# A transformer block in split fp32: the weights' low parts are no longer made, and the flags that skip their products come from the raw weights

## Chip, cores and metric

One NeuronCore of a Trainium2 chip runs the whole program. The metric is device time in microseconds from launch to end; three runs of the kernel before stand in the table further down. Engines are called by these names: TensorE (PE, with its weight loads as PEld), VectorE (DVE), ScalarE (ACT), GpSimd (POOL), SyncE (SP, which here only issues transfers).

## The reference

Eight sequences of 256 tokens of width 128 pass through an attention and a gated feed-forward network, each with a layer norm before and after:

```python
x = x + layernorm(attention(layernorm(x), W_qkv))          # one head of width 128
h = silu(z @ w1.T * s1) * (z @ w2.T * s2)                   # z = layernorm(x); 128 -> 512
h = gelu(h @ h1.T * sh1)                                    # 512 -> 512, exact gelu
h = gelu(h @ h2.T * sh2)                                    # 512 -> 512
x = x + layernorm(h @ w3.T * s3)                            # 512 -> 128
```

All data is fp32. The five weight matrices of the feed-forward network hold only -1, 0 and 1; their scales are separate vectors.

## The kernel before

The 2048 tokens are 16 tiles of 128, in four blocks of four tiles (512 tokens). TensorE multiplies at its fast fp32 format (`float32r` in the code), which keeps only the upper bits of an operand. So each fp32 operand is split: `hi` is the value rounded to that format, `lo` is the rest. A product is then hi x hi + hi x lo + lo x hi, accumulated in PSUM.

For the five feed-forward matrices (`w12` is w1 and w2 side by side, then `h1`, `h2`, `w3`) ScalarE makes the `hi` parts by a copy that rounds (`weights_hi`, line 337), and GpSimd makes the `lo` parts by subtraction (`weights_lo`, line 213): one instruction of 1024 columns for `w12`, four of 512 for `h1`, four of 512 for `h2`, one of 512 for `w3`. ScalarE then sums the absolute values of each `lo` matrix by row (`sum_of_lo`, line 343). TensorE adds the rows up (`sum_flags`, line 716), VectorE copies the totals from PSUM (`copy_flags`, line 602), and TensorE reads each total into a register (`read_flag`). Where the register is zero, `ffn_product` jumps over the matmuls with `w_lo`. With weights of -1, 0 and 1 the `lo` parts are all zero, so this branch is never entered with the given inputs.

Each engine has its own list of instructions, written out by hand, and runs it strictly in order; semaphores tie the lists together. What matters around the change is the start, before the four blocks reach a steady rhythm:

- GpSimd: the inverse square roots of the layer norms (line 198) and the `lo` parts of the weights alternate. First the root for block 0's input norm, then `w12`; the root for block 1's, then four slices of `h1`; the root for block 0's attention norm, two slices of `h2`; the root for block 0's second norm, then two slices of `h2` and `w3`.
- VectorE: the statistics of block 0 and 1 (lines 437 to 446), their normalised tiles (456), the `lo` parts of activations (433), the attention output of block 0 (487 to 501), its normalised tiles `xn2` (456 again), the copy of the first two flags (602), then block 0's gates (515, 523).
- ScalarE: the `hi` parts of activations (260, 294) with the `hi` parts of weights and the four sums between them. The sums of `w12` and `h1` stand before block 0's `x2T`; those of `h2` and `w3` stand after block 0's silus and ahead of block 1's exps (270).
- TensorE: `front_transposes(1)`, `attention_transposes(0)`, four filler matmuls, `front_projections(1)`, twelve filler matmuls, `sum_flags(0)`, `x2_transposes(0)`, two flag reads, two fillers, and `up(0)`, the first layer of the network. The fillers (`keep_warm`, line 859) multiply a tile of zeros and exist only to keep TensorE active; their numbers are in `WARM`.

From `up(0)` on, each block runs `up`, `h1_layer`, `h2_layer` and `down`, interleaved with the attention of the following blocks.

Of the kernel before, what the change touches and what calls it, by code (L numbers as in the profile page):

```python
# [7 lines left out]
P = 128  # L8
BATCHES, SEQ, D = 8, 256, 128
# [18 lines left out]
def sandwich_kernel(nc, x, w_attn, w12, h1, h2, w3, scales, out):  # L28
# [9 lines left out]
    with ctx:  # L38
# [17 lines left out]
        wv_hi, wv_lo = sb("wv_hi", [P, D], f32r), sb("wv_lo", [P, D], f32r)  # L56
        w12_hi, w12_lo = sb("w12_hi", [P, 2 * HID], f32r), sb("w12_lo", [P, 2 * HID], f32r)
        h1_hi, h1_lo = sb("h1_hi", [P, KT, HID], f32r), sb("h1_lo", [P, KT, HID], f32r)
        h2_hi, h2_lo = sb("h2_hi", [P, KT, HID], f32r), sb("h2_lo", [P, KT, HID], f32r)
        w3_hi, w3_lo = sb("w3_hi", [P, KT * D], f32r), sb("w3_lo", [P, KT * D], f32r)  # L60
# [4 lines left out]
        lo_abs = sb("lo_abs", [P, KT * HID])  # L65
        lo_sums = sb("lo_sums", [P, 4])
        flags = sb("flags", [1, 4])
# [47 lines left out]
        wv_split, wv_ready = sem("wv_split"), sem("wv_ready")  # L115
        w12_split, w12_ready = sem("w12_split"), sem("w12_ready")
        h1_split, h1_ready = sem("h1_split"), sem("h1_ready")
        h2_split, h2_ready = sem("h2_split"), sem("h2_ready")
        w3_split, w3_ready = sem("w3_split"), sem("w3_ready")
        lo_sums_ready, flags_in_psum, flags_ready = sem("lo_sums_ready"), sem("flags_in_psum"), sem("flags_ready")  # L120
        chain = sem("vector_chain")
# [65 lines left out]
        def _(pool):  # L187
# [69 lines left out]
        def _(act):  # L257
# [88 lines left out]
            LO_COLUMNS = (2 * HID, KT * HID, KT * HID, KT * D)  # L346
            S_BANK = (A[3], A[0])
# [18 lines left out]
            h1_weights_hi((3,))  # L366
            sum_of_lo(W12, w12_lo[:, :], w12_ready, 1)
# [3 lines left out]
            sum_of_lo(H1, h1_lo[:, :, :].rearrange("p k o -> p (k o)"), h1_ready, KT)  # L371
# [3 lines left out]
            sum_of_lo(H2, h2_lo[:, :, :].rearrange("p k o -> p (k o)"), h2_ready, KT)  # L375
            sum_of_lo(W3, w3_lo[:, :], w3_ready, 1)
            for b in range(BLOCKS):
# [304 lines left out]
        def _(pe):  # L682
# [8 lines left out]
            def ffn_product(n, groups, hi_ready=None, lo_ready=None):  # L691


                last_slice = len(groups[0][1]) - 1
                for k in range(last_slice + 1):
                    if hi_ready:
                        pe.wait_ge(*hi_ready(k))
                    for out, terms in groups:
                        nc.tensor.matmul(out, terms[k][0], terms[k][2], start=(k == 0), stop=False)  # L699
                with pe.If(flag[n] != 0):  # L700
                    for out, terms in groups:
                        for _, w_lo, x_hi, _ in terms:
                            nc.tensor.matmul(out, w_lo, x_hi, start=False, stop=False)
                last = []
                for i, (out, terms) in enumerate(groups):
                    for k, (w_hi, _, _, x_lo) in enumerate(terms):
                        if lo_ready and i == 0:
                            pe.wait_ge(*lo_ready(k))
                        mm = nc.tensor.matmul(out, w_hi, x_lo, start=False, stop=(k == last_slice))  # L709
                    last.append(mm)  # L710
                return last

            def sum_flags(group, out):
                pe.wait_ge(lo_sums_ready, FLAG_GROUPS[group][1])
                c = slice(*FLAG_GROUPS[group])
                nc.tensor.matmul(out[0:1, c], ones[:, :], lo_sums[:, c], start=True, stop=True).then_inc(flags_in_psum, 1)
# [77 lines left out]
            def up(b, slices):  # L794
                pe.wait_ge(x2T_ready, b + 1)
                for o in slices:
                    if o >= 2:
                        pe.wait_ge(a1_full, KT * b + o - 1)
                    elif b > 0:
                        pe.wait_ge(a3_full, KT * (b - 1) + 2 * o + 2)  # L800
                    columns = [slice(m * HID + o * P, m * HID + (o + 1) * P) for m in range(2)]
                    ffn_product(W12, [(F[2 * (o % 2) + m][:, :], [(w12_hi[:, c], w12_lo[:, c], x2T_hi[:, :], x2T_lo[:, :])])
                                      for m, c in enumerate(columns)])[-1].then_inc(up_in_psum, 1)

            def hidden(b, slices, flag_n, w_hi, w_lo, x_hi, x_lo, bank_free, hi_sem, lo_done, done):
                groups = []
                for o in slices:
                    pe.wait_ge(*bank_free(o))
                    c = slice(o * P, (o + 1) * P)
                    groups.append((F[o][:, :], [(w_hi[:, k, c], w_lo[:, k, c], x_hi[:, k, :], x_lo[:, k, :]) for k in range(KT)]))  # L810
                first = slices[0] == 0
                for last in ffn_product(flag_n, groups, (lambda k: (hi_sem, KT * b + k + 1)) if first else None,
                                        (lambda k: lo_done(b, k)) if first else None):
                    last.then_inc(done, 1)

            def down(b):
                pe.wait_ge(gT_ready, min(b + 3, BLOCKS))
                ffn_product(W3, [(A[1][:, :], [(w3_hi[:, k * D:(k + 1) * D], w3_lo[:, k * D:(k + 1) * D], a3_hi[:, k, :], a3_lo[:, k, :])
                                               for k in range(KT)])],
                            lambda k: (a3_hi_ready, KT * b + k + 1), lambda k: a3_lo_done(b, k))[0].then_inc(yT_in_psum, 1)  # L820

            def last_h2_slice(g):
                c, o = slice(g * SEQ, (g + 1) * SEQ), slice((KT - 1) * P, KT * P)
                pe.wait_ge(a2_full, KT * BLOCKS)
                ffn_product(H2, [((F[3], A[3])[g][:, c], [(h2_hi[:, k, o], h2_lo[:, k, o], a2_hi[:, k, c], a2_lo[:, k, c])
                                                    for k in range(KT)])])[0].then_inc(h2_in_psum, 1)

            def last_down(g):
                c = slice(g * SEQ, (g + 1) * SEQ)
                ffn_product(W3, [(A[(1, 0)[g]][:, c], [(w3_hi[:, k * D:(k + 1) * D], w3_lo[:, k * D:(k + 1) * D],  # L830
                                                        a3_hi[:, k, c], a3_lo[:, k, c]) for k in range(KT)])],
# [17 lines left out]
            def h1_layer(b, slices):  # L849
                hidden(b, slices, H1, h1_hi, h1_lo, a1_hi, a1_lo, lambda o: (a1_full, KT * b + 3 + o // 2),  # L850
                       a1_hi_ready, a1_lo_done, h1_in_psum)

            def h2_layer(b, slices):
                hidden(b, slices, H2, h2_hi, h2_lo, a2_hi, a2_lo, lambda o: (a2_full, KT * b + o + 1),
                       a2_hi_ready, a2_lo_done, h2_in_psum)
# [103 lines left out]
```

## Time and profile before

| | |
|---|---|
| time, median of 3 runs | 163.86 us (163.35 to 164.72) |
| span of the profiled execution | 160.3 us |
| TensorE busy | 137.1 us, 86% |
| VectorE busy | 123.2 us, 77% |
| ScalarE busy | 90.7 us, 57% |
| GpSimd busy | 81.1 us, 51% |

The span runs from the first to the last instruction that the profiler records; of the profiled execution only this span is known, and the median of the timed runs is 3.6 us above it. A busy share is an average over the whole span; the start has shares and limits of its own, so it is read by its timeline.

### The profile page before, as it was taken

The page shows a single profiled execution, that of the slowest core. Times are in us where ns is not written, and L with a number is a line of the kernel's source. Part 1 is how long each engine was busy: PE and PEld are TensorE (multiplying, and loading weights), DVE is VectorE, ACT ScalarE, POOL GpSimd, SP SyncE. Part 2 cuts the span into 40 slices and gives each one's busy share as a digit, 9 for nine tenths or more (in the row PEclk, how much of TensorE's full clock was granted, in tenths as well). Part 3 has the DMA queues.
Part 4 walks back from the last instruction along what each step waited for, and adds up shares of the span by engine and source line. Part 5 has one row for each costly group of instructions (what it writes and reads, how often), then busy time and mean ns, then how long its engine had stood idle before and what let it go on. Part 6 is the DMA issues. An engine that isn't in the chain of part 4 may idle for free. (4 is left out here: it accounts for less than half of the span.)

```text
span 160.3 us, 2214 instructions
## 1 busy us (share of the span) xinstructions
PE 137.1 (86%) x676; PEld 102.1 (64%) x676; DVE 123.2 (77%) x337; ACT 90.7 (57%) x157; POOL 81.1 (51%) x73
## 2 busy tenths in 40 slices
PE   6996859868999799999998979999978598979850
PEld 2564636345768587687886847869766385856740
DVE  1777678938979989689769796894697788695864
ACT  3057677455998345847875428678834555463420
POOL 3249339905424846363275672632948745273521
PEclk9999997799999999999999999999999999999999
DMA  4997000000000000000000010000000100001001
GB/s 141 267 359 265 0 4 2 0 0 0 2 0 4 0 0 0 0 4 2 0 0 4 2 65 0 0 4 0 0 0 7 60 6 0 0 0 65 4 0 65
DMA packets 3837, 5.35 MB, mean 33 GB/s; under 512 B 368, under 2 KB 2544, under 8 KB 3824
## 3 DMA queue, kind: packets, MB, share of 16 engines
q1 hardware_dynamic: 3824, 5.19, 9.7%
q8 instruction: 7, 0.11, 0.3%
q14 instruction: 6, 0.05, 0.1%
HBM read 4.14 MB, written 1.05 MB: 32 GB/s over the span
## 5 line engine op out<-in xcount | busy, mean ns | idle before, releaser
L203 POOL TENSOR_TENSOR a_lo<-act_full,a_hi 128x512 fp32r<-128x512 f32 x34 | 45.4, 1343 | 35.6 <-DVE a_hi L523 29.7
L699 PE MATMUL F<-a_hi,h_hi 128*128 128x512 f32 (+1 forms) x128 | 36.3, 405 | 4.8 <-DVE a_hi L523 4.5
L312 ACT ACTIVATE act_full<-F,sc 128x512 f32<-128x512 f32 x31 | 21.0, 689 | 26.2 <-PE F L709 26.2
L523 DVE CAST a_hi<-act_full 128x512 fp32r<-128x512 f32 x47 | 28.3, 609 | 7.4 <-ACT act_full L312 6.4
L709 PE MATMUL F<-a_lo,h_hi 128*128 128x512 f32 (+1 forms) x128 | 33.5, 392 | 0.4 <-DVE a_lo L433 0.4
L699 PEld LDWEIGHTS F<-a_hi,h_hi 128*128 128x128 f32 x128 | 22.3, 189 | 12.1 <-DVE a_hi L523 8.0
L198 POOL TENSOR_TENSOR rstd<-ve,minus_half 128x4 f32<-128x4 f32 x15 | 15.8, 1055 | 24.7 <-DVE ve L557 8.9
L709 PEld LDWEIGHTS F<-a_lo,h_hi 128*128 128x128 f32 x128 | 23.7, 188 | 6.3 <-DVE a_lo L433 0.8
L859 PE MATMUL F<-warm 128*128 128x512 bf16 x50 | 15.8, 467 | 1.9 <-POOL warm L188 1.3
L515 DVE SCALAR_TENSOR_TENSOR act_full<-F,sc,silu 128x512 f32<-128x512 f32 x16 | 11.9, 746 | 5.1 <-ACT silu L306 5.1
L306 ACT ACTIVATE silu<-F,sc 128x512 f32<-128x512 f32 x16 | 10.8, 689 | 6.4 <-PE F L709 6.3
L456 DVE TENSOR_SCALAR xn<-x,mv,rstd 128x128 f32<-128x128 f32 x16 | 11.9, 804 | 2.9 <-POOL rstd L198 2.9
L433 DVE TENSOR_TENSOR a_lo<-act_full,a_hi 128x512 fp32r<-128x512 f32 (+1 forms) x15 | 12.3, 821 | 1.8 <-DVE a_hi L523 0.5
L699 PE MATMUL F<-x2T_hi,w_hi 128*128 128x512 f32 x32 | 10.7, 415 | 2.8 <-DVE x2T_lo L433 2.2
L213 POOL TENSOR_TENSOR h_lo<-h_raw,h_hi 128x512 fp32r<-128x512 f32 x8 | 10.1, 1275 | 5.2 <-ACT h_hi L337 5.2
L859 PEld LDWEIGHTS F<-warm 128*128 128x128 bf16 x50 | 5.5, 117 | 8.7 <-issue 5.1
L709 PE MATMUL F<-x2T_lo,w_hi 128*128 128x512 f32 x32 | 10.0, 395 | 0.0
L270 ACT ACTIVATE probs<-A,neg_max 128x256 f32<-128x256 f32 x16 | 7.4, 472 | 3.3 <-DVE neg_max L465 3.3
L699 PEld LDWEIGHTS F<-x2T_hi,w_hi 128*128 128x128 f32 x32 | 5.4, 188 | 5.9 <-DVE x2T_lo L433 3.8
L433 DVE TENSOR_TENSOR pT_lo<-A,pT_hi 128x512 fp32r<-128x512 f32 x8 | 5.3, 689 | 2.9 <-ACT pT_hi L260 2.9
L437 DVE BATCH_NORM_STATS2 stats<-A 128x6 f32<-128x128 f32 x28 | 6.2, 283 | 1.6 <-PE A L785 1.6
L709 PEld LDWEIGHTS F<-x2T_lo,w_hi 128*128 128x128 f32 x32 | 6.0, 188 | 1.4
(120 smaller groups left out, 244.2 us busy)
## 6 DMA issues: line engine op xcount, KB each, us to landing
h_raw<-h SPq DMA_DIRECT2D x2, 1024.0 KB, 8.9
xs<-x SPq DMA_DIRECT2D x4, 256.0 KB, 6.3
out<-outs SPq DMA_DIRECT2D x3, 256.0 KB, 2.1
w_raw<-w SPq DMA_DIRECT2D x1, 512.0 KB, 5.4
w_raw<-w SPq DMA_DIRECT2D x1, 256.0 KB, 9.9
out<-outs SPq DMA_DIRECT2D x2, 128.0 KB, 1.7
wa_raw<-w_attn SPq DMA_DIRECT2D x1, 192.0 KB, 2.7
sc<-scales SPq DMA_DIRECT2D x1, 8.5 KB, 5.1
```

The costliest lines, as they stand in the source:

```text
L198: nc.gpsimd.tensor_tensor(rstd[:, ln, :], ve[:, ln, :], minus_half[:, :], ALU.pow).then_inc(rstd_ready[ln], 1)
L203: nc.gpsimd.tensor_tensor(dst[:, o, :], act_full[:, o, :], hi[:, o, :].bitcast(f32), ALU.subtract).then_inc(done, 1)
L213: nc.gpsimd.tensor_tensor(lo, raw, hi.bitcast(f32), ALU.subtract).then_inc(done, 1)
L306: nc.scalar.activation(silu1[:, o % 2, :], F[2 * (o % 2)][:, :], ACT.Silu, scale=sc[:, S_W1 + o:S_W1 + o + 1]).then_inc(silu_ready, 1)
L312: nc.scalar.activation(act_full[:, o, :], F[o][:, :], ACT.Gelu, scale=sc[:, first_scale + o:first_scale + o + 1]).then_inc(done, 1)
L433: nc.vector.tensor_tensor(dst, full, hi.bitcast(f32), ALU.subtract).then_inc(done, 1)
L456: nc.vector.tensor_scalar(dst[:, t, :], src(t), mv[:, ln, t, 0:1], rstd[:, ln, t:t + 1], ALU.subtract, ALU.mult).then_inc(done, 1)
L515: nc.vector.scalar_tensor_tensor(act_full[:, o, :], F[2 * (o % 2) + 1][:, :], sc[:, S_W2 + o:S_W2 + o + 1], silu1[:, o % 2, :], ALU.mult, ...
L523: nc.vector.tensor_copy(hi[:, o, :], act_full[:, o, :]).then_inc(hi_sem, 1)
L699: nc.tensor.matmul(out, terms[k][0], terms[k][2], start=(k == 0), stop=False)
L709: mm = nc.tensor.matmul(out, w_hi, x_lo, start=False, stop=(k == last_slice))
L859: nc.tensor.matmul(F[3][:, :], warm[:, 0:P], warm[:, :], start=True, stop=True)
```

## The change

- The tiles `w12_lo`, `h1_lo`, `h2_lo`, `w3_lo` and the ten GpSimd subtractions that filled them are gone. GpSimd's list keeps its inverse square roots in the same order.
- ScalarE no longer sums absolute values of `lo` tiles. It reads the raw fp32 weights as 16-bit integers, every second one (the lower half of each word), copies them as numbers into a scratch tile, and accumulates the sum by row. These four instructions stand where the old four stood, have as many elements, and wait for the weights' transfer in place of GpSimd.
- The branch that is skipped now holds matmuls in plain fp32 on the raw weights, starting the accumulation anew, in place of `float32r` matmuls on `w_lo`.
- TensorE waits for the `hi` parts explicitly before it reads a flag.

```diff
-            def weights_lo(lo, raw, hi, split, n, done):
-                pool.wait_ge(split, n)
-                nc.gpsimd.tensor_tensor(lo, raw, hi.bitcast(f32), ALU.subtract).then_inc(done, 1)
-            def h2_weights_lo(slices):
-                for k in slices:
-                    weights_lo(h2_lo[:, k, :], h2_raw[:, k, :], h2_hi[:, k, :], h2_split, k + 1, h2_ready)
             rsqrt(LN_X, 0)
-            weights_lo(w12_lo[:, :], w12_raw[:, :], w12_hi[:, :], w12_split, 1, w12_ready)
             rsqrt(LN_X, 1)
-            for k in range(KT):
-                weights_lo(h1_lo[:, k, :], h1_raw[:, k, :], h1_hi[:, k, :], h1_split, k + 1, h1_ready)
             rsqrt(LN_O, 0)
-            h2_weights_lo((0, 1))
             rsqrt(LN_X1, 0)
-            h2_weights_lo((2, 3))
-            weights_lo(w3_lo[:, :], w3_raw[:, :], w3_hi[:, :], w3_split, 1, w3_ready)
...
-            def sum_of_lo(n, lo, ready, count):
-                act.wait_ge(ready, count)
+            def sum_of_low_bits(n, raw, columns, loaded):
+                act.wait_ge(loaded, 16)
                 if n > 0:
-                    act.wait_ge(lo_sums_ready, n)
-                nc.scalar.activation(lo_abs[:, 0:LO_COLUMNS[n]], lo, ACT.Abs,
-                                     accum_out=lo_sums[:, n:n + 1]).then_inc(lo_sums_ready, 1)
+                    act.wait_ge(low_sums_ready, n)
+                low_half = raw.bitcast(mybir.dt.uint16).rearrange("p (n h) -> p n h", h=2)[:, :, 0]
+                nc.scalar.activation(low_bits[:, 0:columns], low_half, ACT.Copy,
+                                     accum_out=low_sums[:, n:n + 1]).then_inc(low_sums_ready, 1)
...
                 with pe.If(flag[n] != 0):
                     for out, terms in groups:
-                        for _, w_lo, x_hi, _ in terms:
-                            nc.tensor.matmul(out, w_lo, x_hi, start=False, stop=False)
+                        for k, (_, w_raw, x_hi, _) in enumerate(terms):
+                            nc.tensor.matmul(out, w_raw, x_hi.bitcast(f32), start=(k == 0), stop=False, skip_group_check=True)
...
             def read_flag(n):
+                pe.wait_ge(*((w12_split, 1), (h1_split, KT), (h2_split, KT), (w3_split, 1))[n])
                 pe.wait_ge(flags_ready, (1, 1, 2, 2)[n])
                 flag[n] = pe.value_load(flags[0:1, n:n + 1].bitcast(mybir.dt.int32))
```

## Rows read from the trace of the kernel before

**Rows 1.** The page: span, busy time, clock granted in 40 slices (9 is full).
```profile
span 160.3 us, 2214 instructions
PE 137.1 (86%) x676; PEld 102.1 (64%) x676; DVE 123.2 (77%) x337; ACT 90.7 (57%) x157; POOL 81.1 (51%) x73
...
PEclk9999997799999999999999999999999999999999
```

**Rows 2.** Groups by shape, first 45 us: count | busy us, mean ns | idle.
```profile
L213 POOL TENSOR_TENSOR h_lo<-h_raw,h_hi 128x512 fp32r<-128x512 f32 x8 | 10.1, 1275 | 5.2 <-ACT h_hi L337 5.2
...
L343 ACT ACTIVATE lo_abs<-h_lo 128x2048 f32<-128x2048 f32 x2 | 3.8, 1908 | 0.0
...
L343 ACT ACTIVATE lo_abs<-w_lo 128x1024 f32<-128x1024 f32 x1 | 1.0, 1047 | 0.0
```

**Rows 3.** Timeline of VectorE in the start: start us, duration us, line, operation.
```profile
4.85 0.17 DVE L446 TENSOR_SCALAR ve<-mv 128x4 f32<-128x4 f32 x1
...
6.17 1.12 DVE L456 TENSOR_SCALAR xn<-xs,mv,rstd 128x128 f32<-128x128 f32 x4 [0.69 <-POOL rstd L198]
...
10.95 1.48 DVE L446 TENSOR_SCALAR ve<-mv 128x4 f32<-128x4 f32 x1
...
18.73 2.09 DVE L456 TENSOR_SCALAR xn<-xs,mv,rstd 128x128 f32<-128x128 f32 x4
...
23.02 0.76 DVE L487 TENSOR_TENSOR ve<-mv,eps_s 128x4 f32<-128x4 f32 x1
...
28.67 3.99 DVE L456 TENSOR_SCALAR xn<-x,mv,rstd 128x128 f32<-128x128 f32 x4
```

**Rows 4.** Timeline of GpSimd in the start.
```profile
10.02 2.38 POOL L213 TENSOR_TENSOR w_lo<-w_raw,w_hi 128x1024 fp32r<-128x1024 f32 x1 [3.89 <-ACT w_hi L337]
...
22.50 1.26 POOL L213 TENSOR_TENSOR h_lo<-h_raw,h_hi 128x512 fp32r<-128x512 f32 x1 [2.52 <-ACT h_hi L337]
...
28.60 2.49 POOL L213 TENSOR_TENSOR h_lo<-h_raw,h_hi 128x512 fp32r<-128x512 f32 x2
31.05 1.27 POOL L213 TENSOR_TENSOR w_lo<-w_raw,w_hi 128x512 fp32r<-128x512 f32 x1
```

**Rows 5.** Timeline of TensorE in the start, and two later rows.
```profile
5.13 2.74 PE L859 MATMUL F<-warm 128*128 128x512 bf16 x10
...
13.07 0.39 PE L688 MATMUL A<-xT_hi,gT_hi 128*128 128x256 f32 x1 [1.05 <-DVE gT_lo L433]
...
24.43 0.50 PE L688 MATMUL A<-xT_hi,qk_hi 128*128 128x512 f32 x1 [1.93 <-DVE xT_lo L433]
...
26.60 4.37 PE L859 MATMUL F<-warm 128*128 128x512 bf16 x12
30.90 0.19 PE L716 MATMUL F<-lo_sums,ones 128*1 128x2 f32 x2
...
32.46 0.58 PE L791 MATMUL A<-ident,xn 128*128 128x128 f32 x2 [0.90 <-DVE xn L456]
...
34.46 0.73 PE L699 MATMUL F<-x2T_hi,w_hi 128*128 128x512 f32 x2 [0.19 <-DVE x2T_lo L433]
...
45.36 0.66 PE L770 MATMUL A<-ident,probs 128*128 128x128 f32 x4
...
126.88 0.73 PE L699 MATMUL F<-x2T_hi,w_hi 128*128 128x512 f32 x2 [1.47 <-DVE x2T_lo L433]
```

**Rows 6.** Stretches: length, busy us (count) by engine, granted clock, DMA share, GB/s.
```profile
27.00:28.00 1.00, 1.00 (x4) 0.40 (x3) 0.97 (x6) 1.00 (x2) 0.72 (x2) 0.50 0.00 0
```

**Rows 7.** Timeline of ScalarE.
```profile
27.39 1.90 ACT L343 ACTIVATE lo_abs<-h_lo 128x2048 f32<-128x2048 f32 x1
...
44.28 0.47 ACT L270 ACTIVATE probs<-A,neg_max 128x256 f32<-128x256 f32 x1
```

**Rows 8.** The page's DMA queues: packets, MB, share of 16 engines' span.
```profile
q8 instruction: 7, 0.11, 0.3%
```

**Rows 9.** TensorE's waits for nothing that the profile shows: total, times, longest.
```profile
PE F L859 <- issue: 0.6, 1, 0.6
```

More of the change, by code:

```diff
@@ L56, in sandwich_kernel @@
         wv_hi, wv_lo = sb("wv_hi", [P, D], f32r), sb("wv_lo", [P, D], f32r)
[L57 to L60, printed above, removed]
+        w12_hi = sb("w12_hi", [P, 2 * HID], f32r)
+        h1_hi, h2_hi = sb("h1_hi", [P, KT, HID], f32r), sb("h2_hi", [P, KT, HID], f32r)
+        w3_hi = sb("w3_hi", [P, KT * D], f32r)
         ident = sb("ident", [P, P])
@@ L374, in _ @@
             silus(0, range(KT))
-            sum_of_lo(H2, h2_lo[:, :, :].rearrange("p k o -> p (k o)"), h2_ready, KT)
-            sum_of_lo(W3, w3_lo[:, :], w3_ready, 1)
+            sum_of_low_bits(H2, h2_raw[:, :, :].rearrange("p k o -> p (k o)"), KT * HID, h2_loaded)
+            sum_of_low_bits(W3, w3_raw[:, :], KT * D, w3_loaded)
             for b in range(BLOCKS):
@@ L713, in sum_flags @@
             def sum_flags(group, out):
-                pe.wait_ge(lo_sums_ready, FLAG_GROUPS[group][1])
+                pe.wait_ge(low_sums_ready, FLAG_GROUPS[group][1])
                 c = slice(*FLAG_GROUPS[group])
-                nc.tensor.matmul(out[0:1, c], ones[:, :], lo_sums[:, c], start=True, stop=True).then_inc(flags_in_psum, 1)
+                nc.tensor.matmul(out[0:1, c], ones[:, :], low_sums[:, c], start=True, stop=True).then_inc(flags_in_psum, 1)
             def read_flag(n):
+                pe.wait_ge(*((w12_split, 1), (h1_split, KT), (h2_split, KT), (w3_split, 1))[n])
                 pe.wait_ge(flags_ready, (1, 1, 2, 2)[n])
@@ L801, in up, with hidden @@
                     columns = [slice(m * HID + o * P, m * HID + (o + 1) * P) for m in range(2)]
-                    ffn_product(W12, [(F[2 * (o % 2) + m][:, :], [(w12_hi[:, c], w12_lo[:, c], x2T_hi[:, :], x2T_lo[:, :])])
+                    ffn_product(W12, [(F[2 * (o % 2) + m][:, :], [(w12_hi[:, c], w12_raw[:, c], x2T_hi[:, :], x2T_lo[:, :])])
                                       for m, c in enumerate(columns)])[-1].then_inc(up_in_psum, 1)
-            def hidden(b, slices, flag_n, w_hi, w_lo, x_hi, x_lo, bank_free, hi_sem, lo_done, done):
+            def hidden(b, slices, flag_n, w_hi, w_raw, x_hi, x_lo, bank_free, hi_sem, lo_done, done):
                 groups = []
@@ L809, in hidden @@
                     c = slice(o * P, (o + 1) * P)
-                    groups.append((F[o][:, :], [(w_hi[:, k, c], w_lo[:, k, c], x_hi[:, k, :], x_lo[:, k, :]) for k in range(KT)]))
+                    groups.append((F[o][:, :], [(w_hi[:, k, c], w_raw[:, k, c], x_hi[:, k, :], x_lo[:, k, :]) for k in range(KT)]))
                 first = slices[0] == 0
@@ L824, in last_h2_slice @@
                 pe.wait_ge(a2_full, KT * BLOCKS)
-                ffn_product(H2, [((F[3], A[3])[g][:, c], [(h2_hi[:, k, o], h2_lo[:, k, o], a2_hi[:, k, c], a2_lo[:, k, c])
+                ffn_product(H2, [((F[3], A[3])[g][:, c], [(h2_hi[:, k, o], h2_raw[:, k, o], a2_hi[:, k, c], a2_lo[:, k, c])
                                                     for k in range(KT)])])[0].then_inc(h2_in_psum, 1)
@@ L829, in last_down @@
                 c = slice(g * SEQ, (g + 1) * SEQ)
[L830 removed]
+                ffn_product(W3, [(A[(1, 0)[g]][:, c], [(w3_hi[:, k * D:(k + 1) * D], w3_raw[:, k * D:(k + 1) * D],
                                                         a3_hi[:, k, c], a3_lo[:, k, c]) for k in range(KT)])],
@@ L849, in h1_layer @@
             def h1_layer(b, slices):
-                hidden(b, slices, H1, h1_hi, h1_lo, a1_hi, a1_lo, lambda o: (a1_full, KT * b + 3 + o // 2),
+                hidden(b, slices, H1, h1_hi, h1_raw, a1_hi, a1_lo, lambda o: (a1_full, KT * b + 3 + o // 2),
                        a1_hi_ready, a1_lo_done, h1_in_psum)
             def h2_layer(b, slices):
-                hidden(b, slices, H2, h2_hi, h2_lo, a2_hi, a2_lo, lambda o: (a2_full, KT * b + o + 1),
+                hidden(b, slices, H2, h2_hi, h2_raw, a2_hi, a2_lo, lambda o: (a2_full, KT * b + o + 1),
                        a2_hi_ready, a2_lo_done, h2_in_psum)
```

18 lines of the change are left out of this document (7 added, 11 removed).

## The prediction

> **What bounds the kernel now.** The page comes first: TensorE is busy for 86% of the span [rows 1], but this share is a mean over two very different parts. The next view is the timeline, engine by engine, of the first 45 us, because everything that the diff touches executes there, apart from the bodies of branches that are never entered. Behind `up(0)` nothing changes but ScalarE's two later sums and those bodies.
>
> In the start it is no engine's throughput that decides but one dependent chain through VectorE, GpSimd, ScalarE and TensorE, which ends at the first matmul of `up(0)` at 34.46 us [rows 5]. The reader should go back along it. `up(0)` waited for `x2T_lo`, that for the second pair of transposes at 32.46, and these had waited 0.90 us for VectorE's normalised tiles `xn2` [rows 5]. Those four instructions took 3.99 us [rows 3]; the same four shapes took 1.12 us at 6.17, when GpSimd was in none of its long subtractions [rows 3]. During the slow ones GpSimd was making two slices of `h2_lo` and then `w3_lo`, from 28.60 to 32.32, and the last of the four ended just behind that [rows 4]. The same pattern stands at three more places: a 128x4 `ve` of 1.48 us against 0.17 us [rows 3], ending with `w12_lo` at 12.40 [rows 4]; the tiles of block 1 at 18.73, 2.09 us in place of 1.12; and a `ve` at 23.02 of 0.76 us, ending at 23.78 beside a slice of `h1_lo` that ends at 23.76 [rows 3, 4]. So VectorE is held off while GpSimd subtracts, and GpSimd's subtractions sit on the path although nobody waits for their results.
>
> **Part 1: ten subtractions go.** By themselves they are 8 x 1.275 + 2.38 + 1.27 = 13.9 us of GpSimd [rows 2, 4], none of it awaited directly. What counts is the VectorE time they cost, and how much of each saving reaches the chain.
>
> At 10.95: `ve` shrinks by 1.31 us. `gT_lo` stands behind it and then becomes bound by ScalarE's `gT_hi`, whose end leaves it some 0.9 us earlier; TensorE's scores, which began at 13.07 after waiting 1.05 us for `gT_lo` [rows 5], come 0.9 us sooner, and the maxima, held a little by `v_lo`, 0.77 us sooner. Running total: 0.8 us.
>
> At 18.73: the tiles start 0.77 us sooner and take 0.97 us less. What comes late next is the attention output `oT`, itself 0.77 us sooner; behind it `attention_transposes(0)` start at about 19.75, against 21.04 before. Running total: 1.3 us.
>
> At 23.02: `ve` shrinks by 0.76 - 0.17 = 0.59 us. `xT_lo`, and so block 1's projections at 24.43 [rows 5], and the inverse square root move together. Running total: 1.9 us; projections at 22.55.
>
> At 28.67: GpSimd's root for the second norm would now end at about 26.75, and the four tiles take 1.12 us: they end at 27.9 instead of 32.66. That is 4.8 us, but not all of it reaches `up(0)`, since TensorE's own list has things in between: the projections (2.2 us, so to 24.7), twelve fillers, then `sum_flags(0)`, which needs ScalarE's sum over `h1`. The sum: ScalarE is through its list sooner too. Before, the sum of `h1` began at 27.39 [rows 7], behind `v_hi`, which waits for the projections; these are 1.9 us sooner, so 25.5, if ScalarE has done the rest of its list by then. From 19.1, when the attention product ends, that rest is three copies of 0.6 us, the sum of `w12` (1.05 us [rows 2] and its read), four `h2_hi` slices (2.2 us) and `gT_hi` (0.6): 5.7 us, to 24.8. The sum of `h1` then ends at 27.5. So it is the fillers that end last.
>
> The fillers are the term with two ends. Before, the twelve took 4.37 us [rows 5], because the granted clock fell in the 26th microsecond and came back at about 29.65: it reads 0.50 at 27 to 28 us [rows 6], and the page's line of the clock has its only dip there [rows 1]; that is the 1.2 GHz level, then 2.4 GHz again. It fell after TensorE had stood still for 1.93 us, waiting for `xT_lo` [rows 5]. At the full clock ten of these fillers took 2.74 us [rows 5], so twelve would take 3.2. After the change that stand-still shrinks to about 1.3 us (fillers end at 21.2, projections start at 22.55). The clock survived a stand-still of 1.47 us before 126.88 and the 1.05 before 13.07 [rows 5]; 1.3 lies between those two. I take it that the clock holds: fillers to about 28.0, flags and all four transposes 28.1 to 28.8, then as before `x2T_hi` (0.6) and `x2T_lo` (0.7), and `up(0)` at 30.2. **That is 4.2 us sooner.** The other end, the clock falling as before: fillers to 29.1, `up(0)` at 31.1, 3.3 us sooner. With all twelve fillers at the lower level it is some 2.3 us: twice the ideal 0.21 of 512 columns at 2.4 GHz is 0.43 each, 5.2 together, and `up(0)` starts at 32.1. The two flag reads and fillers behind the transposes (0.63 us [rows 9] and 0.6 us) end at about 30.0 and stay just hidden under `x2T`.
>
> **Part 2: the four sums in 16-bit form.** The same number of elements, in the same places. No row shows an ACT instruction that reads 16-bit data or every second element. Nearest are the old sums, 1.908 us for 2048 columns or 0.93 ns a column, and the exps, the dearest per column, 0.47 us for 256 or 1.84 ns [rows 2, 7]. I take the first, since a copy and a sum of equal columns cost ScalarE the same before (1.05 us for 1024 [rows 2]) and the fixed part of a short exp doesn't grow with columns. Below nothing: a halved rate per column would save 0.9 us ahead of block 1's exps. The dear end: 1.9 us more before `sum_flags(0)` and 1.0 before that make `up(0)` start at 31.9, and another 2.5 us stand ahead of block 1's exps at 44.28 [rows 7], whose transposes TensorE takes up at 45.36 with no gap to spare [rows 5].
> The Trainium skill ("ScalarE: Activation LUTs", section "What ACT_TABLE_LOAD costs") gives one element per cycle and lane for fp32 and bf16 alike, 0.833 ns; by it the sums cost what they cost now. No row here tests it on 16-bit input.
>
> **Part 3: waits.** The sums now wait for loads that landed before 16 us, `read_flag` for `hi` parts that ScalarE had made long before. Behind the sum of `h2` stand only `w3`'s sum and the exps. Cost nothing; the cover is that the transfers are over some 5 us before the first sum.
>
> **Part 4: the body of the skipped branch.** TensorE passes 46 such branches. In the kernel before, two to eight matmuls are jumped over each time, and no gap shows for it: all of TensorE's waits for nothing visible come to 0.6 us, once [rows 9]. A plain fp32 matmul is recorded twice (one call at line 716, count 2 [rows 5]), so the 184 skipped matmuls may become 368 with as many weight loads. I take nothing, as the longest body before cost no more than the shortest.
>
> **The sum.** 34.46 - 30.2 = 4.2 us, and from `up(0)` on nothing in the lists depends on absolute time: all loads are done, and every wait is on the other engines, which shift along. 160.3 - 4.2 = 156.1 us of span, and with the 3.6 us around it 159.7 us; against the median, 163.86 - 4.2 = 159.7 us, the same.
>
> **Rivals.**
> *The clock falls anyway*, or in another place. For it: ahead of the new stand-still of 1.3 us lie transposes, another short gap and only four fillers, where the 1.47 us before 126.88 had dense matmuls around it. Then `up(0)` gains 2.3 to 3.3 us: 160.6 to 161.6 us.
> *The saving is mostly covered:* 16-bit sums at the exps' rate. `up(0)` is 2.6 us sooner, and 2.5 us are given back at block 1's exps: 163.8 us, no change. Against it: equal prices of ScalarE's plain copies and sums.
> *The longer code is felt:* the mechanism is the fetch of TensorE's instructions across a jump. The row of one instruction queue has 7 packets in 0.3% of 16 engines' span, so 0.003 x 16 x 160.3 / 7 = 1.1 us each [rows 8]. Today none is visible [rows 9]. If jumps over bodies twice as long left the stretch already fetched, each uncovered fetch would cost 1.1 us; four eat up the gain, and with six the time is 159.7 + 6.6 = 166.3 us, slower.
> The Trainium skill ("Runtime: NRT & Kernel Launch", section "Instruction fetch mechanics") says that a taken branch whose target is outside the fetched window stalls on the fetch; this rule speaks against the change. That the old jumps cost nothing speaks for targets inside that window.
> *It doesn't do what it says:* if something other than GpSimd's subtractions stretches VectorE, the 2.8 us at 28.67 stays and `up(0)` gains under 1 us: 163 us. The four coincidences of ends speak against it.
>
> **Chances.** Forecast, clock held: 0.57 (159.2 to 160.4). Clock falls: 0.25. Dear sums or no effect: 0.08. Code fetch: 0.05 (0.04 of it slower). More than forecast, under 159.0, for instance by faster sums: 0.05. A measurement of this kernel tells about 1%, 1.6 us, from no change. Faster by over 1% (under 162.2): 0.87; within: 0.09; slower: 0.04. The range 158.9 to 161.9 leaves out the last three cases and the edge of the second.
>
> **What would show it.** In the profile after: `ve` at line 446 and 487 under 0.2 us; both groups of four tiles in 1.1 us; the transposes of `x2` unbroken, right behind the fillers; the granted clock at full in the 20s; sums at 1.9 us per 2048 columns; `up(0)` near 30.2 us, and every later stage the same distance earlier. Wrong would be: waits of TensorE for nothing visible, just behind the first matmuls of `ffn_product`; a clock of 0.5 for more than 3 us; or a later stage that stretches.

## The result and the profile after

The changed kernel takes 158.89 us, median of 4 runs (158.61 to 159.44), against 163.61 us for 4 runs of the kernel before (162.17 to 164.72). The ratio is 0.9695 with a 95% interval of 0.9649 to 0.9741; it is taken from undisturbed executions only and so isn't the quotient of the two medians, which are 4.7 us apart. The kernel is faster, as forecast; the median lies 0.01 us under the range, and the forecast of 4.2 us was too small.

The time is the span plus 1.7 to 1.9 us in the executions of either kernel for which both are known (159.44 and 157.7 in the profiled one). So the profiled execution of the kernel before, with its span of 160.3 us, was one of about 162.1 us, well under that kernel's median. This becomes important below.

The head of the page after, to be held against [rows 1]:

```profile
span 157.7 us, 2208 instructions
PE 136.7 (87%) x676; PEld 102.4 (65%) x676; DVE 117.2 (74%) x337; ACT 90.5 (57%) x157; POOL 67.4 (43%) x63
...
PEclk9999999999999999999999999999999599999998
```

GpSimd has 10 instructions and 13.7 us less. VectorE has the same 337 instructions and is busy for 6.0 us less: its work didn't change, only how long it was held. The dip of the clock at a sixth of the span is gone, and a new one stands at about 124 us.

The timeline of VectorE in the start, against [rows 3]:

```profile
11.52 0.17 DVE L429 TENSOR_SCALAR ve<-mv 128x4 f32<-128x4 f32 x1
...
18.52 1.11 DVE L439 TENSOR_SCALAR xn<-xs,mv,rstd 128x128 f32<-128x128 f32 x4
...
22.35 0.16 DVE L470 TENSOR_TENSOR ve<-mv,eps_s 128x4 f32<-128x4 f32 x1
...
27.41 1.12 DVE L439 TENSOR_SCALAR xn<-x,mv,rstd 128x128 f32<-128x128 f32 x4
```

1.48, 2.09, 0.76 and 3.99 us became 0.17, 1.11, 0.16 and 1.12: all four stretches went at once. TensorE's timeline answers to [rows 5]:

```profile
8.28 0.60 PE L713 MATMUL A<-ident,xn 128*128 128x128 f32 x4
...
23.17 0.50 PE L671 MATMUL A<-xT_hi,qk_hi 128*128 128x512 f32 x1 [1.33 <-DVE xT_lo L416]
...
25.27 2.76 PE L843 MATMUL F<-warm 128*128 128x512 bf16 x12
28.15 0.19 PE L699 MATMUL F<-low_sums,ones 128*1 128x2 f32 x2
28.27 0.66 PE L775 MATMUL A<-ident,xn 128*128 128x128 f32 x4
29.76 0.59 PE L843 MATMUL F<-warm 128*128 128x512 bf16 x2 [0.83 <-issue]
30.34 0.73 PE L682 MATMUL F<-x2T_hi,w_hi 128*128 128x512 f32 x2
```

The stand-still ahead of the projections is 1.33 us instead of 1.93, the clock held behind it, and the four transposes of `x2` follow one another right behind the fillers. `up(0)` starts at 30.34 us. The fillers were through 0.5 us before VectorE's last tile, at 28.53 us, and both hand over to the same four transposes. From the end of the last tile to `up(0)` it is 1.8 us in either kernel (28.53 to 30.34 here, 32.66 to 34.46 before), so at the end of the start TensorE's list and VectorE's chain are level.

A start time by itself isn't the right measure, since the first x transposes, the same work in both kernels, began at 8.28 us here and at 7.70 before:

```profile
7.70 0.60 PE L729 MATMUL A<-ident,xn 128*128 128x128 f32 x4
```

Measured from them, `up(0)` comes after 22.06 us, against 26.76: **the change takes 4.70 us out of the start.** From `up(0)` to the end of the span it is 127.4 us here and 125.8 before. These 1.5 us go where the clock fell, behind a wait of TensorE that both traces have. Timeline, and a stretch with its granted clock as last figure but two:

```profile
122.75 1.22 PE L682 MATMUL F<-x2T_hi,w_hi 128*128 128x512 f32 x2 [1.47 <-DVE x2T_lo L416]
```

```profile
124.00:125.00 1.00, 1.00 (x3) 0.76 (x3) 0.71 (x1) 0.14 (x1) 0.16 (x1) 0.50 0.10 25
```

The sums on 16-bit data, grouped by shape, cost to the nanosecond what the old ones cost [rows 2]:

```profile
L327 ACT ACTIVATE low_bits<-h_raw 128x2048 f32<-128x2048 uint16 x2 | 3.8, 1908 | 0.0
L327 ACT ACTIVATE low_bits<-w_raw 128x1024 f32<-128x1024 uint16 x1 | 1.0, 1047 | 0.0
```

### The profile page after: what moved, and what is told of

Same layout as the page of the kernel before. It is cut to its first block and busy times, and to the rows that moved or that the text cites. A ratio compares the mean times of both kernels' runs of the same rounds, so it can differ in the third digit from the quotient of the medians.

```text
span 157.7 us, 2208 instructions
## 1 busy us (share of the span) xinstructions
PE 136.7 (87%) x676; PEld 102.4 (65%) x676; DVE 117.2 (74%) x337; ACT 90.5 (57%) x157; POOL 67.4 (43%) x63
## 5 line engine op out<-in xcount | busy, mean ns | idle before, releaser
L506 DVE CAST a_hi<-act_full 128x512 fp32r<-128x512 f32 x47 | 27.9, 600 | 7.5 <-ACT act_full L294 6.3
L843 PE MATMUL F<-warm 128*128 128x512 bf16 x50 | 14.4, 432 | 2.1 <-POOL warm L184 1.3
L682 PE MATMUL F<-x2T_hi,w_hi 128*128 128x512 f32 x32 | 11.6, 446 | 2.6 <-DVE x2T_lo L416 2.0
L439 DVE TENSOR_SCALAR xn<-x,mv,rstd 128x128 f32<-128x128 f32 x16 | 9.0, 625 | 2.9 <-POOL rstd L194 2.9
L692 PE MATMUL F<-x2T_lo,w_hi 128*128 128x512 f32 x32 | 10.8, 420 | 0.0
L682 PEld LDWEIGHTS F<-x2T_hi,w_hi 128*128 128x128 f32 x32 | 5.9, 205 | 5.8 <-DVE x2T_lo L416 3.6
L692 PEld LDWEIGHTS F<-x2T_lo,w_hi 128*128 128x128 f32 x32 | 6.6, 206 | 1.6
L423 DVE BATCH_NORM_AGGREGATE mv<-stats 128x2 f32<-128x6 f32 x60 | 5.7, 158 | 0.5
```

Source lines behind the costliest of these rows:

```text
L439: nc.vector.tensor_scalar(dst[:, t, :], src(t), mv[:, ln, t, 0:1], rstd[:, ln, t:t + 1], ALU.subtract, ALU.mult).then_inc(done, 1)
L506: nc.vector.tensor_copy(hi[:, o, :], act_full[:, o, :]).then_inc(hi_sem, 1)
L843: nc.tensor.matmul(F[3][:, :], warm[:, 0:P], warm[:, :], start=True, stop=True)
```

## The experiments

Twelve more runs were made, in three sets of four, each set on another chip. The two numbers that tell most are read from TensorE's timeline in each profile: from the first x transposes to `up(0)` ("start"), and from `up(0)` to the end of the span ("rest"). "Falls" are the stretches at a clock of 0.5 behind the start (two of them begin 0.5 and 0.8 us ahead of `up(0)`). Those of the last 5 us of a span aren't listed, since TensorE's last matmul is over by then.

| kernel | start | rest | falls, us | median of its runs (range) | ratio to the kernel before |
|---|---|---|---|---|---|
| before, first profile | 26.76 | 125.8 | none | | |
| before, again | 26.75 | 128.3 | 93 to 97, 128 to 131 | 164.31 (one run) | |
| before, third | 26.74 | 129.6 | 34 to 37, 95 to 98, 129 to 133 | 166.23 (one run) | |
| changed, first profile | 22.06 | 127.4 | 122 to 126 | 158.89 | 0.9695 |
| changed, again | 22.06 | 127.3 | 122 to 126 | 159.0 (156.66 to 159.56) | 0.964 |
| subtractions back | 26.75 | 129.6 | 34 to 38, 96 to 99, 130 to 133 | 166.27 (165.9 to 166.5) | 1.0138 |
| last three back | 25.10 | 127.1 | 32 to 36 | 161.34 (161.1 to 165.42) | 0.9829 |
| last three late | 25.43 | 127.3 | 125 to 129 | 162.25 (162.02 to 162.49) | 0.9908 |
| short bodies | 22.03 | 127.2 | 122 to 125 | 159.32 (158.81 to 159.69) | 0.9719 |
| changed, four fillers | 22.38 | 125.8 | none | 157.64 (156.96 to 159.34) | 0.9613 |
| changed, more fillers | 22.07 | 125.8 | none | 156.93 (156.81 to 159.2) | 0.9571 |
| before, four fillers | 27.58 | 125.9 | none | 162.19 (161.74 to 163.11) | 0.9912 |
| before, more fillers | 27.25 | 125.8 | none | 163.79 (161.85 to 165.18) | 0.9958 |
| changed, delayed | 26.94 | 127.5 | 127 to 131 | 163.84 (162.12 to 165.25) | 0.9964 |

In each set the kernel before ran alongside, with medians of 164.33, 164.62 and 164.41 us. Some of the intervals of the ratios are given below.

The start isn't free of what lies ahead of it. The x transposes begin between 6.91 and 8.37 us in the fourteen profiles. In four of them (last three back, changed with four fillers, before with four fillers, delayed) ScalarE then waited for the transfer of the scales, which adds 0.2 to 0.55 us to their start: the attention transposes came 0.18, 0.32, 0.55 and 0.47 us later behind the x transposes than in their twins.

**The changed kernel again.**

> The changed kernel once more, unaltered, as the measure for its neighbours. Theory A (the profile of the first run): its start is 4.1 us shorter than before, and about 1.5 us are lost again where the clock falls behind TensorE's wait of 1.47 us at 122.75 us. If that fall is a matter of luck, the executions differ by about 1.5 us in span, and most lie at 156.7 to 157.7 us; theory B (it falls in every execution, since the wait is always there): spans within 0.5 us and a mean clock of 0.986 or 0.987 each time. Time against before: ratio 0.965 to 0.975.

159.0 us in 6 runs, ratio 0.964 (0.9551 to 0.973), which is 5.3 us under the 164.33 of its neighbours. Theory B describes it better, though not to the letter: five spans of six lie between 156.9 and 157.8, which is 0.9 us apart and not 0.5, and the second profile has the same fall in the same place. But one execution ended at 156.66 us (span 154.9), so the fall isn't certain.

**The ten subtractions back.** Nothing reads their results and nothing waits for them; ScalarE's sums, the waits and the longer branch bodies stay as changed. The tiles and the two helpers, without their semaphores, return too.

```diff
             rsqrt(LN_X, 0)
+            weights_lo(w12_lo[:, :], w12_raw[:, :], w12_hi[:, :], w12_split, 1)
             rsqrt(LN_X, 1)
+            for k in range(KT):
+                weights_lo(h1_lo[:, k, :], h1_raw[:, k, :], h1_hi[:, k, :], h1_split, k + 1)
             rsqrt(LN_O, 0)
+            h2_weights_lo((0, 1))
             rsqrt(LN_X1, 0)
+            h2_weights_lo((2, 3))
+            weights_lo(w3_lo[:, :], w3_raw[:, :], w3_hi[:, :], w3_split, 1)
```

> The changed kernel with the ten GpSimd subtractions put back in their old places of GpSimd's list; nothing reads their results, and nothing waits for them. Output is the reference's. Theory A (VectorE is held off while GpSimd subtracts, and that is the whole gain): the time of the kernel before, ratio to it 0.995 to 1.005; first matmul of up(0) within 0.5 us of 34.5 us; the four xn2 tiles take 4.0 us and the ve at 10.95 takes 1.5 us. Rival C (the gain is in what ScalarE no longer waits for, or in the 16-bit sums): it stays at the changed kernel's time, ratio 0.97, up(0) near 30.3 us.

The start is 26.75 us again, within 0.01 us of the kernel before (`up(0)` itself stands at 35.12 us, 0.12 beyond the expected bound, as the x transposes began at 8.37). TensorE's rows, and VectorE's with the old durations:

```profile
8.37 0.60 PE L729 MATMUL A<-ident,xn 128*128 128x128 f32 x4
...
35.12 1.29 PE L698 MATMUL F<-x2T_hi,w_hi 128*128 128x512 f32 x2
```

```profile
11.62 1.47 DVE L445 TENSOR_SCALAR ve<-mv 128x4 f32<-128x4 f32 x1
...
19.39 2.10 DVE L455 TENSOR_SCALAR xn<-xs,mv,rstd 128x128 f32<-128x128 f32 x4
...
23.69 0.76 DVE L486 TENSOR_TENSOR ve<-mv,eps_s 128x4 f32<-128x4 f32 x1
...
29.34 3.98 DVE L455 TENSOR_SCALAR xn<-x,mv,rstd 128x128 f32<-128x128 f32 x4
```

So the whole gain in the start comes from the ten subtractions; rival C is out. That they act by holding VectorE is read from its durations. There is a second way, by GpSimd's own list, where the root of a layer norm stands behind a subtraction. In the kernel before each of the three roots concerned begins 0.07 to 0.08 us behind its `ve` (12.50, 23.86 and 27.63 us), so none was late by the list alone. But the slice beside the `ve` at 23.02 ended at 23.76 us, and the root would have had to wait for it even behind a short `ve`; for this root the two ways can't be told apart, for the `xn2` tiles they can (next experiments).

The time is 1.0138 of the kernel before (1.0084 to 1.0192), above what was expected. Its rest is 129.6 us with three falls, as in the third profile of the kernel before, and all its six runs are in that group (spans 164.1 to 164.7), where only some of that kernel's are (two of 11 in this set, 14 of 39 in all three, from 164.0 us up). Why all six fall into this group isn't shown.

**The last three back.** Only `h2_weights_lo((2, 3))` and `w3`'s subtraction return, behind the last root of the start.

```diff
             rsqrt(LN_X1, 0)
+            h2_weights_lo((2, 3))
+            weights_lo(w3_lo[:, :], w3_raw[:, :], w3_hi[:, :], w3_split, 1)
```

> The changed kernel with only the last three subtractions put back (two slices of h2 and w3, behind the inverse root of block 0's second norm). Theory A, by the terms of the prediction: the start keeps its gains at 10.95, 18.73 and 23.02 (1.9 us together) and loses that at 28.67, so up(0) starts at about 32.3 us, 2 to 2.3 us later than in the changed kernel; the xn2 tiles take 4.0 us. Time: 1 to 3 us above the changed kernel's, the spread being where the clock falls. If instead it is the wait of GpSimd's roots behind subtractions in its own list that counts, up(0) stays near 30.3 us, since none of the three stands ahead of a root of the start.

The `xn2` tiles take 3.99 us again, and `up(0)` begins 3.04 us later behind the x transposes than in the changed kernel, more than the 2 to 2.3 expected. The tiles are 2.87 us longer and 0.18 us are the wait for the scales. The expectation was too small because it took 22.5 us for the changed kernel's start, by the terms of the prediction, where 22.06 was measured. The three earlier stretches keep 26.75 - 25.10 = 1.65 us. None of the three subtractions stands ahead of a root of the start, so here it is the holding of VectorE alone.

**The last three late.** All ten are back, but the last three wait until VectorE is through with `xn2`. Beside the lines of "the ten subtractions back" there is one wait:

```diff
             rsqrt(LN_X1, 0)
+            pool.wait_ge(xn2_ready, TB)
+            h2_weights_lo((2, 3))
+            weights_lo(w3_lo[:, :], w3_raw[:, :], w3_hi[:, :], w3_split, 1)
```

> The changed kernel with all ten subtractions back, the last three of them only behind the fourth xn2 tile (GpSimd waits for it). GpSimd has the work of the kernel before. Theory A: the four xn2 tiles take 1.1 us and not 4.0, the three earlier stretches stay, so up(0) starts 23.9 us behind the first x transposes, against 26.75 before and 22.06 in the changed kernel; time 160 to 162.5 us. If GpSimd's load as such slowed VectorE's stage, up(0) would stay at 26.75.

VectorE behaves as expected, with the work of the kernel before on GpSimd:

```profile
23.15 0.77 DVE L487 TENSOR_TENSOR ve<-mv,eps_s 128x4 f32<-128x4 f32 x1
...
28.80 1.11 DVE L456 TENSOR_SCALAR xn<-x,mv,rstd 128x128 f32<-128x128 f32 x4
```

But the start is 25.43 us, not 23.9. TensorE's timeline shows why:

```profile
26.70 4.44 PE L860 MATMUL F<-warm 128*128 128x512 bf16 x12
31.07 0.19 PE L716 MATMUL F<-low_sums,ones 128*1 128x2 f32 x2
31.19 0.66 PE L792 MATMUL A<-ident,xn 128*128 128x128 f32 x4
```

The tiles were ready at 29.9 us, and the transposes had to wait for fillers at half clock (0.50 from 27 to 30 us). In the kernel before the same dip lay under VectorE's long tiles and cost nothing (its third profile has no dip there and the same start); as soon as these are short, it is on the path. In the changed kernel the stand-still ahead is 1.33 us, and the clock held in each of the six profiles that have this wait.

**Short bodies.** The branch that is skipped gets matmuls of the old form, with the `hi` parts in place of the `lo` parts that no longer exist.

```diff
-                        for k, (_, w_raw, x_hi, _) in enumerate(terms):
-                            nc.tensor.matmul(out, w_raw, x_hi.bitcast(f32), start=(k == 0), stop=False, skip_group_check=True)
+                        for w_hi, _, x_hi, _ in terms:
+                            nc.tensor.matmul(out, w_hi, x_hi, start=False, stop=False)
```

> The changed kernel with the old form of matmul in the branch that is skipped (float32r, the high parts standing in for the low ones; never executed with these inputs, so the output is the reference's). Theory A: the same time as the changed kernel within 0.3 us, as no wait of TensorE stands behind a branch in the profile. Rival D (the longer code costs something, hidden in small steps): 1 us or more faster than the changed kernel, and one packet less in the instruction queue, 7 in place of 8.

159.32 us against 159.0; start and rest are the changed kernel's within 0.15 us. The queue of instructions shows that the code did grow by the change, by one packet. First the changed kernel, then this one:

```profile
q8 instruction: 8, 0.13, 0.4%
```

```profile
q8 instruction: 7, 0.11, 0.3%
```

**Fillers ahead of block 3**, in the changed kernel and in the kernel before:

```diff
                     x2_transposes(b + 1)
+                    for _ in range(4):
+                        nc.tensor.matmul(A[1][:, :], warm[:, 0:P], warm[:, :], start=True, stop=True)
```

> The changed kernel with four filler matmuls into the idle bank A1 in the wait of 1.47 us ahead of block 3's first layer, where the clock fell in the profiled run. Theory A: the clock holds there; the step from up(0) to the end is 125.8 us as in the kernel before instead of 127.4, so span 155.0 to 156.0 us and 1.0 to 1.5 us faster than the changed kernel where that one's clock falls. Rival E (the clock then falls at another of the waits of about 1 us, or the fillers delay the layer): no gain, or up to 0.5 us slower.

> The kernel before with four filler matmuls into bank A1 ahead of block 3's first layer and nothing else, as was done to the changed kernel, which it made 1.3 us faster. Theory F: of the two falls behind up(0) in the usual profile (at 94 and at 128 us) the second goes and the first stays, 0.7 to 1.3 us faster than the kernel before, ratio 0.992 to 0.996. If the first goes with it, or none, the wait isn't what decides.

The changed kernel's median is 1.4 us under its twin's of the same set (157.64 and 159.0), and five of its six spans lie between 155.1 and 156.3 us, five of the twin's between 156.9 and 157.8. The intervals of the two ratios overlap nearly whole, though (0.9550 to 0.9677 and 0.9551 to 0.973). Its rest is 125.8 us, as expected. In its profile the wait shows as 0.61 us in place of 1.47, and the clock holds:

```profile
120.70 0.81 PE L903 MATMUL A<-warm 128*128 128x512 bf16 x3
122.12 0.73 PE L682 MATMUL F<-x2T_hi,w_hi 128*128 128x512 f32 x2 [0.61 <-DVE x2T_lo L416]
```

The kernel before gains 2.2 us by the medians and 1.4 by the ratio (0.9912, 0.9877 to 0.9947), against 0.7 to 1.3 expected; by the times alone it could be one fall. But in its profile the fall at 94 us is gone too, though it stands 30 us ahead of the new fillers, and all six of its spans lie between 159.9 and 161.3 us, where only two of 39 of the unaltered kernel do. By the condition set beforehand, the wait ahead of block 3 isn't all that decides, and what removes the earlier fall stays open.

**More fillers**, in both kernels: four more ahead of block 1's projections, three ahead of the flag reads, and the four ahead of block 3; in the kernel before also three behind each of the first three `xn2` transposes.

```diff
-WARM = (8, 10, 6, 4, 4, 4, 12, 2)
+WARM = (8, 10, 6, 4, 4, 8, 12, 2)
...
+            keep_warm(3)
             read_flag(W12)
```

> The kernel before with more filler matmuls in TensorE's waits: four more ahead of block 1's projections (8 in place of 4), three behind each of the first three xn2 transposes of block 0, three ahead of the flag reads, four into bank A1 ahead of block 3's first layer. No step of the chain through VectorE changes. Theory F: the clock holds in most executions, mean 0.985 or more, span 159 to 160.5 us, which is 2 us under the usual kernel before and still 4 us above the changed kernel with fillers. Theory G: the time of the kernel before.

> The changed kernel with the same additional fillers, but for those between the xn2 transposes, which follow one another there. Theory F: span 155 to 156 us, and 4.0 to 4.6 us less than the kernel before with its fillers: this is the chain through VectorE without the clock, 4.1 us in the first two profiles. Compared with the changed kernel 1 to 1.5 us faster, about as with four fillers ahead of block 3 alone.

The two profiles are the cleanest pair, both with a rest of 125.8 us. Their starts are 5.18 us apart, of which 0.5 is what the fillers between the transposes cost the kernel before. Their spans, 160.2 and 155.6, are 4.6 us apart, as the x transposes began 0.62 us later in the changed one. But in most of its 12 runs the kernel before wasn't so: spans of 161.3 to 163.4, and a median of 163.79 (ratio 0.9958, 0.9913 to 1.0003). Theory F asked for 159 to 160.5 in most, and got two. The changed kernel with these fillers is the fastest of all: 156.93 us, ratio 0.9571 (0.9503 to 0.9638).

**The changed kernel, delayed.** The last number of `WARM`, the fillers right ahead of `up(0)`, goes from 2 to 24.

```diff
-WARM = (8, 10, 6, 4, 4, 4, 12, 2)
+WARM = (8, 10, 6, 4, 4, 4, 12, 24)
```

> The changed kernel with 22 more filler matmuls right ahead of up(0) (24 in place of 2, 0.216 us each, so 4.75 us), at which TensorE stays busy. From up(0) on every list is the changed kernel's, only as late as in the kernel before: first matmul 26.8 us behind the first x transposes. Theory F1 (where the clock falls depends on when TensorE's waits come, so the earlier start is worth more than itself): as in the usual kernel before, two falls behind up(0), 128 us from up(0) to the end, span 162 to 162.7, ratio to the kernel before 0.995 to 1.003. Theory F2 (the kernel before loses the clock more often for another reason, such as its sparse work from 30 to 34 us): one fall behind up(0), 127.4 us to the end, span 161.3 or less, ratio 0.988 to 0.994.

Inconclusive between the two: the profile has one fall and a span of 161.3 (F2), the median of 163.84 and the ratio of 0.9964 (0.9903 to 1.0025) lie where F1 wants them, and the six spans run from 160.2 to 163.4. One thing is settled: 4.75 us put ahead of `up(0)` cost 4.8 us against the 159.0 of the changed kernel (measured in the first set), and bring back the time of the kernel before within the interval. So the 4.7 us of the start are worth about themselves. Whether fewer falls give a further part isn't settled: the delayed kernel is still 0.6 us under its neighbours by the medians, and its interval allows from 1.6 us faster to 0.4 slower.

**The kernel before, twice more.**

> The kernel before once more, for one profile. Ten of its timed executions had a mean granted clock of 0.956 to 0.967 and a span of 161.5 to 164.7 us; the profile on which the prediction rests had 0.987 and 160.3 us. Theory F (the clock decides the difference, and the kernel before usually loses it where TensorE's work is on the path): if this profile is one of the usual ones, up(0) starts within 0.7 us of 34.5 us, and the clock is at 0.5 in two or three stretches behind it, that together cost 2 us. Theory G (the usual execution differs in its start, say by later transfers): up(0) later by 2 us.

> The kernel before, one more profile, to see whether the falls of the clock stand in the same places as in the last one. Theory F: span 162.4 to 162.7 with falls at 92 to 97 and 128 to 132 us; if it is one of the executions at 164, a third stretch at half clock lies on the path, in one of block 1's or 2's dense stretches.

The start is the same three times (26.74 to 26.76 us). The rest is 125.8, 128.3 and 129.6 us. Stretches of the second profile:

```profile
94.00:95.00 1.00, 1.00 (x4) 0.80 (x3) 1.00 (x3) 0.60 (x1) 1.00 (x1) 0.50 0.00 0
129.00:130.00 1.00, 1.00 (x4) 0.81 (x3) 0.61 (x2) 0.69 (x1) 0.00 (x0) 0.50 0.06 16
```

and of the third:

```profile
35.00:36.00 1.00, 1.00 (x4) 0.81 (x4) 0.00 (x0) 0.38 (x1) 0.00 (x0) 0.50 0.00 0
97.00:98.00 1.00, 1.00 (x4) 0.80 (x3) 0.77 (x2) 0.00 (x0) 1.00 (x2) 0.50 0.00 0
131.00:132.00 1.00, 1.00 (x4) 0.75 (x3) 0.35 (x1) 0.69 (x1) 0.00 (x0) 0.50 0.09 25
```

Theory F holds, G is out; but the third stretch of the last profile, expected in block 1 or 2, lies right at block 0's `up(0)`. It follows the long `xn2` tiles, between whose transposes TensorE stands still for 0.9 us at a time. A fall there, at 32 to 38 us, is in three profiles (this one, the subtractions back, the last three back), in which these tiles took 4 us and the clock had held at 25 us. In three others with long tiles the clock had fallen at 25 us and held here, in a fourth fillers stood between the transposes and it held too; in the seven profiles with short tiles there is none. So the long tiles may cost some executions such a fall besides their own length; what this is worth in the median isn't measured. Among the 39 timed executions of this kernel beside the three sets only two have a clock of 0.987 and a span of 160.4. The profile that the prediction used was a rare one.

## Why the prediction was right or wrong

**What bounds the kernel now: right.** GpSimd's subtractions lay on the path by holding VectorE, and putting them back restores the start to within 0.01 us.

**Part 1, stretch by stretch.** Counted from the x transposes, the attention transposes came 12.04 us behind them (forecast 12.05) and the projections 14.89 us behind (forecast 14.85). These terms were right. The stretch at 28.67 was, too: `xn2` was ready 20.25 us behind them (forecast 27.9 - 7.70 = 20.2), and the clock held after a stand-still of 1.33 us (forecast 1.3).

**The step that failed is the price of twelve fillers at the full clock.** It was put at 3.2 us, from ten that took 2.74; measured, 2.76. The row was no row at full clock: the same ten fillers took from 2.32 to 3.41 us in the fourteen profiles, all with a recorded clock of 1.00, behind eight that took 3.6, or 0.45 us each, about the pace of the 1.2 GHz level and twice that of the rows below. TensorE was still coming up to speed while they ran. Two later rows of the kernel before had the right price:

```profile
8.14 1.46 PE L859 MATMUL F<-warm 128*128 128x512 bf16 x6
...
14.61 1.04 PE L859 MATMUL F<-warm 128*128 128x512 bf16 x4
```

Two more fillers cost 0.42 us there, so twelve take 2.7. The 0.44 us are all that the start's 4.70 us exceed the 4.26 from 34.46 to 30.2. By 3.2 us the fillers would have ended last; by 2.76 they are level with VectorE's tiles, and shorter ones would have gained no more. In the first pair of profiles the miss was hidden, as the x transposes began 0.58 us later after the change and `up(0)` stood at 30.34 as if the sum had been exact.

**"From `up(0)` on nothing in the lists depends on absolute time" was true of the lists, but the clock is not in them.** The granted clock falls in places that differ from one execution to the next, and a fall on the path costs 1.2 to 1.6 us: rests of 125.8 or 125.9 us with none, 127.1 to 127.5 with one, 128.3 with two, 129.6 with three, in fourteen profiles. The forecast took the clock as a question of the start only. The range, 158.9 to 161.9, had no term for it, although the three times of the kernel before (163.35 to 164.72) already spread by 1.4 us.

**The time around the span** was put at 3.6 us, from a median and a profile that weren't the same execution. It is 1.7 to 1.9. By the profile the forecast should have read 156.1 + 1.8 = 157.9 us, by the median 159.7; that these two disagree would have been the sign that the profile was not a usual one. The 0.8 us from 159.7 to the measured 158.89 are 0.44 of the fillers, 0.06 of rounding 4.26 to 4.2, and 0.25 because a fourth run brought the median of the kernel before from 163.86 to 163.61. So it was chance that the median came out just beyond the edge of the range and not just inside.

Taking the difference to the median was the sounder of the two ways: 163.61 - 4.70 = 158.91 us. That this hits 158.89 so closely is luck in part. The kernel before has two and three falls behind the start in its second and third profile, the changed one has one, and in the next set the same two kernels were 5.3 us apart.

**Part 2: right.** 1908 ns before and after, for 2048 columns; 1047 for 1024, which is 0.84 ns for each further column. The Trainium skill ("ScalarE: Activation LUTs", section "What ACT_TABLE_LOAD costs") states one element per cycle and lane, 0.833 ns, for fp32 and bf16; the trace agrees, and shows the same for 16-bit integers at every second place.

**Parts 3 and 4: right in the sum, which took nothing for them.** One thing did grow: TensorE's wait at the first two flag reads, that no other engine's work explains, is 0.78 to 0.88 us in the eight profiles with the new `read_flag` where nothing stands between it and the transposes, and 0.55 to 0.65 in the four such profiles with the old one. The short bodies don't shorten it (0.82), so it goes with the reads and not with the bodies. It is covered: `up(0)` waits for `x2T_lo`, which is done at 30.28 us.

The rival of the longer code is out: one more packet of instructions, and no time. Its price of 1.1 us a packet would have needed a fetch that TensorE waits for, and the traces show none. The rule of the Trainium skill that the prediction names ("Runtime: NRT & Kernel Launch", section "Instruction fetch mechanics") is that a taken branch stalls if its target lies outside the fetched window; no run here shows such a stall, so none tests it.

**Two slips that don't enter the forecast.** The clock was back at 29.85 us and not at 29.65, as the half microsecond from 29.50 has a mean of 0.65. And with fillers to 29.1 us, the same 2.2 us behind them that the forecast has would put `up(0)` at 31.3 and not at 31.1.

## What to carry to other kernels

Work that nobody waits for can still sit on the critical path: look for instructions of one engine that take several times their usual duration and end just behind an instruction of another (0.02 to 0.34 us here), and cost such work by what it holds off, not by its own busy time. Compare starts of a stage from a common earlier event, not from zero, and take the price of an instruction at full clock only from a stretch that has been at full clock for a while. And set the profiled execution's span against the spread of the timed ones before adding terms to it: if it is a rare one without falls of the clock, a gain that only the usual ones have isn't in it.

## What the runs showed of the hardware

- VectorE's `tensor_scalar` between SBUF tiles, its two-input operation on SBUF tiles and its cast are held by a subtraction on GpSimd (128x4: 0.17 to 1.48 us; 128x512 cast: 0.43 to 0.97 us), while `bn_stats` and operations with one input from PSUM keep their time beside it (0.87 us for four `bn_stats` with and without; the gates' 128x512 product with an input from PSUM, 0.74 beside a subtraction and 0.75 alone). The changed kernel still has such places: its casts of `a_hi` take 0.96 us at 34.20, beside GpSimd's `a_lo`.
- No length of a wait decides by itself whether the clock falls. After 1.47 us it held in two profiles of ten (the first of the kernel before, and the last three back) and fell in eight, both of the changed kernel among them; after 1.93 us it fell in four of six and held in the third of the kernel before and with the subtractions back; after 1.33 us it held in all six profiles that have it. A stretch at the 1.2 GHz level behind such a wait lasted 3.4 us, and once 6.8 (before, four fillers, from 25 to 31 us).
- Four fillers in one wait removed not only the fall behind it but, in the kernel before, one that had stood 30 us earlier in the usual profile. The runs don't show why.
